# Attention and expert kernel: limits made later and spread by way of a DRAM row, x loaded between stored rows, copies of x moved

## What is computed

```python
xn = layernorm(x)
# attention branch, 16 heads of 16
Q, K, V = (lif(layer_norm(xn @ W.T + b, g, beta), 1.0) for W, b, g, beta in (q, k, v))   # 0 or 1
attn = 16 - (q_sum + k_sum.T - 2 * Q @ K.T) + log_pe_bias        # 4096 x 4096 a head, never formed
s = lif(layer_norm(lif(attn * scale @ V, 0.5) @ Wo.T + bo, go, betao), 1.0)
# expert branch
xr = rms_norm(xn) * scale_ffn
ids = argmin(dist2(xr, centroids))                               # one of 8 experts for each row
y = (a * silu(g)) @ down_w[ids],   a, g = split(xr @ up_w[ids])
out = x + s * silu(y + xn)
```

## Time and profile before

| what | value |
|---|---|
| median of three runs | 407.53 us |
| the profiled execution's own time | 409.36 us |
| its span | 407.6 us |
| TensorE busy | 376.3 us, 92% |
| VectorE busy | 325.1 us, 80% |
| ScalarE busy | 225.4 us, 55% |
| GpSimd busy | 219.2 us, 54% |
| chain that ended last | PE 56%, DVE 16%, DMA 11%, issue 8%, ACT 4%, POOL 2% |

### The profile page before, as it was taken

How to read it: one execution, slowest core, us unless ns; L and a number is a source line. 1 busy time by engine, 2 the same in 40 slices (tenths; PEclk the granted TensorE clock), 3 DMA queues, 4 the chain that set the end, 5 groups by cost and what they waited for, 6 DMA issues and landing times.

```text
span 407.6 us, 9980 instructions
## 1 busy us (share of the span) xinstructions
PE 376.3 (92%) x2595; PEld 314.6 (77%) x2596; DVE 325.1 (80%) x824; ACT 225.4 (55%) x613; POOL 219.2 (54%) x291
## 2 busy tenths in 40 slices
PE   4996999999996899999799999999999999999991
PEld 2775888788874687878588788888888888888881
DVE  6676899899977989896777877787888787777873
ACT  4364877877883055341555555555555555555551
POOL 2243777778760023234646676666666666666642
PEclk9998999999998899999999999999999999999998
DMA  7449554957520022042912312323313233332000
GB/s 229 143 137 322 180 166 168 322 170 223 170 93 1 3 78 79 27 139 65 316 52 80 87 51 72 88 82 90 90 58 90 78 87 91 89 90 59 26 15 0
DMA packets 31697, 44.90 MB, mean 110 GB/s; under 512 B 4073, under 2 KB 25762, under 8 KB 31540
## 3 DMA queue, kind: packets, MB, share of 16 engines
q1 hardware_dynamic: 25200, 29.73, 23.2%
q0 software_dynamic: 6240, 14.73, 12.4%
q10 hardware_dynamic: 228, 0.10, 0.1%
HBM read 36.32 MB, written 15.63 MB: 127 GB/s over the span
## 4 chain that ended last, share of the span: by engine, by line
PE 56%; DVE 16%; DMA 11%; issue 8%; ACT 4%; POOL 2%; DVEq 1%; SPq 0%; ACTq 0%; POOLq 0%
PE bank L614 14%; PE bank L444 11%; PE bank L632 11%; DMA row_a<-rows_a,slot_id 7%; PE bank L503 4%; PE bank L597 2%; PE bank L586 2%; ACT d_hi L820 2%; DMA down_sb<-in_down_w 2%; PE bank L367 2%; PE bank L507 2%; PE bank L424 2%; DVE up_lo L1167 2%; DVE d_lo L1209 2%; DVE e_hl L1212 2%
## 5 line engine op out<-in xcount | busy, mean ns | idle before, releaser
L1209 DVE TENSOR_TENSOR d_lo<-down_sb,d_hi 128x1024 fp32r<-128x1024 f32 x39 | 47.9, 1227 | 32.9 <-ACT d_hi L820 32.9
L1338 POOL DMA_INDIRECT row_a<-rows_a,slot_id x39 | 41.6, 1066 | 45.3 <-DVE e_o L1223 42.5
L820 ACT ACTIVATE d_hi<-down_sb 128x1024 fp32r x39 | 41.3, 1060 | 44.4 <-PE bank L632 40.9
L1371 POOL DMA_INDIRECT out_x<-e_o,slot_id x39 | 44.5, 1142 | 20.8 <-issue 14.5
L614 PE MATMUL bank<-up_hi,e_xh 128*128 x156 | 51.8, 413 | 0.2 <-issue 0.2
L614 PE MATMUL bank<-up_hi,e_xl 128*128 x156 | 48.5, 392 | 1.2 <-DVE e_xl L1187 1.2
L1344 POOL DMA_INDIRECT row_s<-rows_s,slot_id x39 | 40.3, 1034 | 15.7 <-issue 11.6
L614 PE MATMUL bank<-up_lo,e_xh 128*128 x156 | 48.5, 392 | 0.0
L771 ACT ACTIVATE junk<-bank 128x256 bf16<-128x256 f32 x32 | 12.0, 383 | 47.6 <-PE bank L537 47.6
L742 ACT ACTIVATE junk<-bank 128x256 bf16<-128x256 f32 x96 | 35.4, 379 | 4.6 <-PE bank L444 4.5
L802 ACT ACTIVATE e_xh<-bank 128x256 fp32r<-128x256 f32 x39 | 15.0, 385 | 39.3 <-PE bank L586 39.3
(11 more groups left out here) (223 smaller groups left out, 1005.7 us busy)
## 6 DMA issues: line engine op xcount, KB each, us to landing
up_raw<-in_up_w SPq DMA_DIRECT2D x16, 512.0 KB, 5.4
rows_a<-xn SPq DMA_DIRECT2D x32, 129.0 KB, 3.1
rows_a<-in_x SPq DMA_DIRECT2D x8, 512.0 KB, 5.0
down_sb<-in_down_w SPq DMA_DIRECT2D x8, 512.0 KB, 5.0
xs<-in_x SPq DMA_DIRECT2D x7, 512.0 KB, 3.5
rows_s<-s_out SPq DMA_DIRECT2D x8, 256.0 KB, 2.5
blk_tab<-in_blocks SPq DMA_DIRECT2D x1, 1024.0 KB, 7.0
row_a<-rows_a,slot_id POOLq DMA_INDIRECT x39, 3.4
```

The costliest lines, as they stand in the source:

```text
L820: act.activation(d_hi[:, :, :], down_sb[:, bass.ds(e, 1), :, :].rearrange("p a c n -> p (a c) n"), ACT.Copy).then_inc(d_high, 1)
L1209: V.tensor_tensor(d_lo[:, :, :], down_sb[:, bass.ds(e, 1), :, :].rearrange("p a c n -> p (a c) n"), d_hi[:, :, :].bitcast(F32), ALU.subtra ...
L1338: G.indirect_dma_start(row_a[s % 4][:, :], None, rows_a, bass.IndirectOffsetOnAxis(ap=slot_id[:, s:s + 1], axis=0), bounds_check=N - 1, oo ...
L1371: G.indirect_dma_start(out, bass.IndirectOffsetOnAxis(ap=slot_id[:, s:s + 1], axis=0), e_o[s % 4][:, :], None, bounds_check=N - 1, oob_is_ ...
```

## The change

Six things are done at once.

- **Limits.** The eight operations leave the start of VectorE. They are seven now (the maximum of -gain and gain is one operation): four stand behind `centred(2)`, three behind the centroids' low part. TensorE's `limits()` and ScalarE's `keep_limits` are gone. GpSimd stores the eight rows to a DRAM array `lim_rows` (4 KB), waits for that, and loads them back as one row repeated over 128 partitions, straight into `thr`. VectorE waits for this load at the first `spikes`.
- **Scale rows.** The matmuls of the ffn scale (L354) stand behind `centre(0)`, and ScalarE makes the first weight's high part before `fs_row`.
- **centred(1)** stands ahead of the first statistics.
- **Sums.** TensorE's `sums()` stands behind `step_a(1, 0)`; VectorE's two copies of them move into `output_bias`.
- **Loads of x.** Groups 1 to 3 are issued ahead of the first stored row; groups 4 to 7 after rows 1, 5, 9 and 13.
- **Copies of x.** The eight copies from x to `rows_a` are issued behind the last stored row.

```diff
@@ SP @@
-            for g in range(1, NT // 4):
+            def load_group(g):
                 sp.wait_ge(x_loaded, 16 * g)
                 load_x(4 * g, 4 * g + 4, x_loaded)
+            for g in range(1, 4):
+                load_group(g)
             for t in range(NT):
                 sp.wait_ge(rms_put, t + 1)
                 sp.dma_start(rows_a[t * P:(t + 1) * P, 0:D + 2], xn[t % 4][:, :]).then_inc(row_put[t % 4], 16)
...
-                if t % 4 == 2:
-                    rows = slice((t - 2) * P, (t + 2) * P)
-                    sp.dma_start(rows_a[rows, D + 2:2 * D + 2], x[rows, :]).then_inc(x_copied, 16)
+                if t % 4 == 1 and t // 4 + 4 < NT // 4:
+                    load_group(t // 4 + 4)
...
+            for g in range(NT // 4):
+                rows = slice(4 * g * P, 4 * (g + 1) * P)
+                sp.dma_start(rows_a[rows, D + 2:2 * D + 2], x[rows, :]).then_inc(x_copied, 16)
@@ TensorE @@
-            for c in range(DC):
-                last = pe.matmul(bank[5][...], ident[0:NV, FS_ + c:...].broadcast_to([NV, P]), vec_raw[:, :], ...)
-            last.then_inc(fs_rows, 1)
...
-            def limits():
-                pe.wait_ge(lim_made, 1)
-                pe.wait_ge(vec_kept, 1)
-                pe.wait_ge(fs_kept, 1)
-                for n in range(8):
-                    last = pe.matmul(bank[4 + n // 4][...], ident[0:8, n:n + 1].broadcast_to([8, P]), lim8[:, 3, :], ...)
-                last.then_inc(lim_rows, 1)
...
-                            pe.wait_ge(thr_kept, 1)
+                            pe.wait_ge(vec_kept, 1)
+                            pe.wait_ge(fs_kept, 1)
...
             centre(0, bank[1])
+            for c in range(DC):
+                last = pe.matmul(bank[5][...], ident[0:NV, FS_ + c:...].broadcast_to([NV, P]), vec_raw[:, :], ...)
+            last.then_inc(fs_rows, 1)
             turn_centroids()
             centre(1, bank[2])
             step_a(0, 0)
-            limits()
             pe.wait_ge(cen_kept, 1)
             centre(2, bank[3])
+            step_a(1, 0)
             sums()
-            step_a(1, 0)
             centre(3, bank[7])
@@ ScalarE @@
+            weights_high(0, bank[1])
             act.wait_ge(fs_rows, 1)
             act.activation(fs_row[:, :], bank[5][:, 0:D], ACT.Copy).then_inc(fs_kept, 1)
             normalize(0, 0)
-            weights_high(0, bank[1])
...
             step_a(0, 0)
-            keep_limits()
@@ VectorE @@
-            V.tensor_scalar(lim8[:, 0, :], gain8, -1.0, None, ALU.mult)
-            V.tensor_scalar(lim8[:, 1, :], beta8[:, :], -1.0 / 16, 1.0 / 16, ALU.mult, ALU.add)
-            row_step(V.tensor_scalar(lim8[:, 2, :], gain8, 0.0, 1e20 / 16, ALU.is_equal, ALU.mult))
-            row_step(V.tensor_tensor(lim8[:, 0, :], lim8[:, 0, :], gain8, ALU.max))
-            row_step(V.tensor_scalar(lim8[:, 0, :], lim8[:, 0, :], 1e-30, None, ALU.max))
-            row_step(V.reciprocal(lim8[:, 3, :], lim8[:, 0, :]))
-            row_step(V.tensor_tensor(lim8[:, 3, :], lim8[:, 1, :], lim8[:, 3, :], ALU.mult))
-            V.tensor_tensor(lim8[:, 3, :], lim8[:, 3, :], lim8[:, 2, :], ALU.subtract).then_inc(lim_made, 1)
...
             centred(0)
+            centred(1)
             for part in range(5):
                 for k in range(2):
                     stats(k, 0, part)
-            centred(1)
             centred(2)
+            dve.wait_ge(ld_beta, 16)
+            row_step = chain(dve, lim_n)
+            V.tensor_scalar(lim8[:, 1, :], beta8[:, :], -1.0 / 16, 1.0 / 16, ALU.mult, ALU.add)
+            V.tensor_scalar(lim8[:, 2, :], gain8, 0.0, 1e20 / 16, ALU.is_equal, ALU.mult)
+            row_step(V.scalar_tensor_tensor(lim8[:, 0, :], gain8, -1.0, gain8, ALU.mult, ALU.max))
+            row_step(V.tensor_scalar(lim8[:, 0, :], lim8[:, 0, :], 1e-30, None, ALU.max))
             dve.wait_ge(cen_turned, 1)
...
+            row_step(V.reciprocal(lim8[:, 3, :], lim8[:, 0, :]))
+            row_step(V.tensor_tensor(lim8[:, 3, :], lim8[:, 1, :], lim8[:, 3, :], ALU.mult))
+            V.tensor_tensor(lim8[:, 3, :], lim8[:, 3, :], lim8[:, 2, :], ALU.subtract).then_inc(lim_made, 1)
             centred(3)
...
-            dve.wait_ge(cen_summed, 1)
-            step(V.tensor_copy(small[:, 88:96], bank[6][:, 8:16]))
-            V.tensor_copy(ny[:, :], bank[6][:, 0:E]).then_inc(ny_kept, 2)
             def output_bias():
+                dve.wait_ge(cen_summed, 1)
+                step(V.tensor_copy(small[:, 88:96], bank[6][:, 8:16]))
+                V.tensor_copy(ny[:, :], bank[6][:, 0:E]).then_inc(ny_kept, 2)
...
                 if k == 0 and n == 2:
-                    dve.wait_ge(thr_kept, 1)
+                    dve.wait_ge(thr_kept, 16)
@@ GpSimd @@
-            for pair in range(2):
-                inverse_stds(pair)
+            inverse_stds(0)
+            pool.wait_ge(lim_made, 1)
+            pool.dma_start(lim_rows, lim8[:, 3, :]).then_inc(lim_put, 16)
+            inverse_stds(1)
+            pool.wait_ge(lim_put, 16)
+            pool.dma_start(thr[:, :], lim_rows.rearrange("a b -> (a b)").unsqueeze(0).broadcast_to([P, 4 * D])) \
+                .then_inc(thr_kept, 16)
             pool.wait_ge(ld_t, 16)
```

More of the change, by code:

```diff
@@ L352, in _ @@
                     last.then_inc(sgn_rows, 1)
-            for c in range(DC):
-                last = pe.matmul(bank[5][:, c * P:(c + 1) * P],
-                                 ident[0:NV, FS_ + c:FS_ + c + 1].broadcast_to([NV, P]), vec_raw[:, :], start=True, stop=True)
-            last.then_inc(fs_rows, 1)
             def centre(p, into):
@@ L476, in _ @@
             centre(0, bank[1])
+            for c in range(DC):
+                last = pe.matmul(bank[5][:, c * P:(c + 1) * P],
+                                 ident[0:NV, FS_ + c:FS_ + c + 1].broadcast_to([NV, P]), vec_raw[:, :], start=True, stop=True)
+            last.then_inc(fs_rows, 1)
             turn_centroids()
@@ L708, in _ @@
             weights_high(1, bank[2])
-            def keep_limits():
-                act.wait_ge(lim_rows, 1)
-                for h in range(2):
-                    last = act.activation(thr[:, 512 * h:512 * h + 512], bank[4 + h][:, :], ACT.Copy)
-                last.then_inc(thr_kept, 1)
             def keep_output_bias():
```

9 lines of the change are left out of this document (3 added, 6 removed).

## The result

Four runs of the changed kernel gave 403.05, 403.72, 404.84 and 402.63 us, median **403.38**; the kernel before, with one more run on that chip, has the median 407.87. The medians differ by 4.5 us. The ratio is 0.988, with a 95% interval of 0.985 to 0.991, which is 4.9 us (3.6 to 6.2); a ratio is worked out apart from the medians and need not be their quotient. The forecast was 401.1, in a range of 399.2 to 404.4. Two later comparisons of the same two kernels on other chips gave ratios of 0.986 (0.982 to 0.990, medians 409.91 and 403.19) and 0.987 (0.984 to 0.991, 409.50 and 404.40).

A forecast was written before the change was run, and what follows sets the result against it. VectorE and TensorE nearly fill the projection loop, so it can only start earlier, after a late first stored row and slow setup. Gains 3.3 + 2.1 + 1.0 = 6.4 us off the median 407.53 give 401.1, range 399.2 to 404.4.

The forecast's parts named there:

- The sum: Whole kernel: setup 3.3, idle 2.1 and clock 1.0 add to 6.4 us gained.
- the terms for idle and clock: Around tile 4: VectorE's idle behind the first stored row gains 2.1 us, TensorE's clock staying full gains 1.0.
- Setup, 3.3 expected: From the start to low part 2: earlier limits, centring and sums bring it 3.3 us forward.
- The 3.60 us of the limits on VectorE's start: VectorE's start: without the limit operations the copy vc can run at 5.51 instead of 9.11, 3.60 us earlier.
- The wait for the sums: VectorE before low part 2: sums ready about 21.8, asked for at 21.5, a new wait of 0.3 us.
- The limits' load, no wait: At spikes(0): limits land between 21.6 and 27.2, read at 26.3; no wait taken, bounds 0 and 0.9 us.
- thinnest cover: The limits' load by way of DRAM before spikes(0), named as the least covered wait of the change.
- (b): Start stays bound: centre(0) at 1.2 GHz takes 6.4 us instead of 3.75; time 403.7 to 404.4; chance 0.09.
- (d): Slower: limits' load takes more than 13 us to land; with 16 us time 409.5 to 410.5; chance 0.05.
- (a): Limits land late, at 28 to 31, VectorE stands at spikes(0); gain 1.7 to 4.7 us; chance 0.14.

The follow-up runs named there:

- after_control: The changed kernel itself, timed again on the chip of the third group; median 404.40, ratio 0.987 to the kernel before.
- loads_only: The kernel before with only x groups 4 to 7 loaded behind rows 1, 5, 9 and 13; median 406.86, ratio 0.994.
- setup_only: The changed kernel with SP's queue as before: all x loads ahead of the first stored row, copies in the loop; median 410.20, ratio 1.001.
- warm_gap: The changed kernel with nine unused matmuls of zeros behind centre(2), in TensorE's idle stretch; median 404.46, ratio 0.989.
- limits_early: The changed kernel with the last three limit operations before the wait for the centroids, limits' load before GpSimd's second factors; median 401.33, ratio 0.982.
- low_first: The changed kernel with VectorE's low parts of weight 1 and tile 0 ahead of the statistics of tiles 2 and 3; median 407.56, ratio 0.995.
- after_again: The changed kernel itself, timed again on the chip of the first group; median 403.19, ratio 0.986 to the kernel before.
- limits_late: The changed kernel with the limits stored twice and their load issued only after GpSimd's first loop step; median 405.46, ratio 0.991.
- limits_tensor: The changed kernel with limits spread by TensorE behind centre(2) and copied by ScalarE, without the DRAM way; median 402.73, ratio 0.984.
- copies_back: The changed kernel with the copies of x back in the loop behind every fourth stored row; median 403.46, ratio 0.986.

## Why the prediction was right, and where its terms were off

**The mechanism held.** Expected, with what the changed kernel's trace shows in brackets:

- centre(0) starts near 6.6 (6.71) and keeps its 3.75 us (3.75); the first low part ends near 18 (17.38);
- low parts 2 and 4 near 25.3 and 31.5 (25.61 and 32.38);
- the store of row 0 is issued near 18.8 (18.06), and the normalisation of tile 4 names no stored row (it names nothing);
- the clock stays full from 30 to 44 (1.00 and 1.00);
- spikes(0) near 26.3 without a wait (26.68; none in three of the four traces with this setup and load order, after_control being the other);
- copies and loop unchanged.

The sum was 6.4, and the loop's end moved by 6.1. The medians moved by 4.5, 6.7 and 5.1 us in the three comparisons, the ratios give 4.9, 5.8 and 5.2. The measured 403.38 lies in the upper part of the range, and the 404.40 of after_control at its end.

**The step from the sum to the median.** I took 6.4 off a median, but the sum was read from one execution that lay 1.5 to 1.8 us above that median. Whether this explains the 1.5 us between the sum and the 4.9 of the first ratio is not shown. The 1.35 us by which that execution was slower in the setup than loads_only don't explain it, since they did not reach its loop's end (setup_only). The intervals of all three ratios hold 6.1 us, and 409.36 is an ordinary time of the kernel before in the three groups (medians 409.16 to 409.91). So no part of the loop's 6.1 us is known to be missing from the timed runs.

**How the 6.1 us divide.** At the loop's end the loads alone gave 3.8 us, where the terms for idle and clock held 3.1; the setup on top of them gave 2.0 to 2.2, where its term held 3.3. But loads_only ran its setup 1.35 us faster than the execution from which the terms were read, and with the wait gone this reaches the loop's end. Laid on that execution, the shares would be about 2.5 and 3.4 to 3.6, an estimate from these numbers. So the line between the two terms moves with an accident of timing. The sum is firmer than its parts, and that 3.3 was met so closely is partly luck.

**Setup, 3.3 expected, 3.24 measured at tile 2, for reasons partly wrong.**

(1) The 3.60 us of the limits on VectorE's start held 0.9 us of the meeting with GpSimd, which I had seen as a row (L868, 0.77 against 0.21) and used only for what it might cost after, not for what it made the kernel before look like. Measured from loads_only, tile 2 gained 1.9 to 2.5 us (27.50 to 25.61, 25.30 and 25.00).

(2) I gave centre(1) its 2.67 us of before and had it start at 11.9. It took 1.99 and started at 11.25, so TensorE was done sooner, and my schedule had the first low part end at 17.9 with TensorE ready at 16.9; in the trace it ends at 17.38 with TensorE ready at 15.2, an idle of 2.33 us. The clock then was 0.50 from 18 to 20, and the projection of tile 0, twelve matmuls that take 2.11 us at the full clock, took 3.33; its piece in the chain of waits:

```profile
18.19 3.33 PE bank L436 x12
```

(3) The wait for the sums, expected at 0.3, was 1.14 for that reason. The rival of a stall that only changes its place was not on my list; warm_gap prices it at about 1.4 us at the loop's end.

**Idle and clock, 2.1 and 1.0.** Tile 4 moved by 4.9 us, 1.7 more than tile 2, against the 2.1 expected: between the two VectorE took 6.77 us where it had worked 6.32 before, and operations of it met GpSimd again. In the changed kernel, for example:

```profile
23.50 0.78 DVE L956 CAST b<-small 128x8 bf16<-128x8 f32 x1
23.53 0.72 POOL L1285 TENSOR_TENSOR sq<-xn,fs_row 128x256 f32<-128x256 f32 x1
...
24.52 0.17 DVE L956 CAST b<-small 128x8 bf16<-128x8 f32 x1
```

This is a meeting ahead of tile 2, where the same cast took 0.78 instead of 0.17; one between the tiles, at 31.39, made an operation of 0.16 us last 0.67, and that is about the difference. They go with what the Trainium skill says in "SBUF — State Buffer", section "Who interferes with whom": VectorE and GpSimd share a port pair that one of the two holds for a whole instruction. The rest of the way to the loop's end gave 1.2 us more, near the 1.0 for the clock; no run changed the clock alone there. ScalarE asked for tile 4 at 30.49 and not at 27.8, so the stored row had more cover than I thought.

**What the form of the sum hid.** I added 3.3 for the setup and 2.1 for the stored row as if each stood for itself. setup_only shows the first is worth nothing without the second. The reason stood in my own text: the first row waits for the last load at 28.79, whatever the setup does.

**The limits' load, no wait.** Right for the profiled execution, with 0.7 us left, and wrong by 0.72 in after_control. As "thinnest cover" it was named. Its bounds, landing 21.6 to 27.2 by rows of stores and copies, hold the landings of the three traces of the changed kernel (25.97, 23.9 and 26.8); with another time of issue it was 19.6 in limits_early and 28.5 in low_first. The 7.9 us that the prediction gives to stored rows belongs to a copy of 512 KB; the stored rows to 60 us took at most 7.4. The Trainium skill's rule against such loads (same page, "SBUF: two separate sides") gave an estimate of 2.5 us of delay. The issues here took 0.60 to 0.65 us in every kernel, amid VectorE's work. The landings of 7.4 and 7.8 us would fit the estimate against the 5.0 of the earlier trace rows, but the windows of the load in the changed kernel and in after_again, third pair VectorE, tell against it:

```profile
18.60:26.00 7.40, 7.40 (x40) 6.39 (x38) 5.59 (x25) 3.93 (x16) 4.36 (x7) 0.86 0.94 255
```

```profile
18.60:26.00 7.40, 7.28 (x49) 6.22 (x48) 6.50 (x29) 5.06 (x21) 4.59 (x8) 1.00 0.70 220
```

VectorE was busy 5.59 us in the first, where the load took 7.4, and 6.50 in the second, where it took 4.8; the DMA engines were busy 0.94 and 0.70. So a busier VectorE did not go with a slower load, and busier DMA engines did. These are two executions, and the busy time does not tell the modes of VectorE apart, so the rule is not refuted by them.

**The rivals.** (b), a start that stays bound, did not occur: centre(0) took 3.75 us. Its price was wrong as well. It multiplied the longest record, 0.795 us, by eight to 6.4, but the records overlap: eight of 0.379 would be 3.03, and a group of such matmuls took 1.99. (d), slower, had no run near it: the longest landing, 8.3 us, is far from 13. (a) came in small in after_control, with 0.72 us, and large only where another order issued the load later (limits_late, low_first).

## What to carry to other kernels

A wait whose end is set by another queue swallows any gain made ahead of it, so ask of each term of a sum what it is worth alone before adding it: here, at the loop's end, 0.1 us for the setup, 3.8 for the loads and 5.9 for both. When a small edit is priced from one trace, look for operations in it that an accident of timing made longer than their like, and ask whether that accident reaches the end of the stage at all: here it made one term too large and moved nothing behind tile 4. Judge the edit by a milestone that the trace repeats, not by a total that spreads more than the edit is worth. Moving work that seems to have no reader behind the critical operation is safe only after asking who waits for it.

## What was not expected of the hardware

- **centre(1) ran in one of two lengths.** In nine of the twelve traces with the changed setup eight matmuls of 128x256 f32 behind the scale rows took 1.99 or 2.00 us; in setup_only, after_again and after_control they took 3.78, as centre(0) does in most traces (3.75), with a granted clock of 1.00 printed for either. The line of after_control, which answers to the one of 1.99 at 11.25 above:

```profile
11.89 3.78 PE L368 MATMUL bank<-w_ctr,w_raw 128*128 128x256 f32 x8
```

  The slow form costs less than it seems. TensorE then has no long idle before tile 1, the clock stays 1.00 from 16 to 20, and tile 2 comes at 25.00 to 25.30, against 25.61 with the fast form and the idle. The length does not belong to centre(1) alone. In the three slow traces the four row matmuls ahead of it took 1.22 us, in the other eight of the twelve that print 1.00 there 0.70 to 0.76, so it looks as if TensorE went over from slow to fast ahead of centre(1) in one case and behind it in the other. That the double length is the lower level of the clock, printed as 1.00, is likely: in limits_tensor, where the record prints 0.50 from 7.3 to 10.6, the row matmuls took 1.14. It is not proven, and what sets the moment is open.
- **The load that repeats a DRAM row** over 128 partitions (512 KB) took from issue to landing: 4.5 us issued at 15.05, 5.0 at 15.61, 6.2 at 18.04, 7.4 at 18.57, 7.8 at 18.98 but 4.8 at 19.08, 8.3 at 20.20, 4.4 at 23.82; in the other three traces with such a load 5.5 at 15.86, 6.2 at 18.43 and 6.0 at 18.98. Size and access are the same in all eleven, so the spread comes from something else, and the traffic of stores, x and expert weights beside it is the likeliest.
- **Zeros kept the clock up, limit rows did not,** over fillings of the same length (2.11 and 2.05 us), in one trace each and with the earlier fall in limits_tensor as a second difference; an idle of 1.2 us in limits_early left it at 1.00, one of 2.33 us in the changed kernel, copies_back and limits_late did not.
